# TensorE's sum over states moved to the front of a step with a lag of two units, and VectorE's gate one unit later

## The reference

```python
h = layernorm(x) @ W_fc1.T + b_fc1
u, z = split(h @ W_in.T)                    # 1024 channels each
u = silu(causal_conv4(u) + conv_b)
dt, B, C = split(u @ W_xproj.T)             # 32, 16, 16
delta = softplus(dt @ W_dt.T + b_dt)
h_t = exp(delta_t * A) * h_(t-1) + (delta_t * u_t) * B_t      # 16 states a channel
y_t = sum_over_states(h_t * C_t) + u_t * D
x = x + ((y * silu(z)) @ W_out.T) @ W_fc2.T + b_fc2
```

## Time and profile before

| | us |
|---|---|
| median of 3 runs | 4184.7 (4183.61 to 4185.17) |
| the profiled execution | 4190.9 |
| its span, from first to last instruction | 4189.1 |
| VectorE busy in it | 3739.9 (89%) |
| TensorE busy, as the profile models it | 3583.6 (86%) |
| GpSimd busy | 3318.2 (79%) |
| ScalarE busy | 2983.0 (71%) |

### The profile page before, as it was taken

One profiled execution on the slowest core, in us unless ns is written; L12 is line 12 of the kernel. 1 busy time (PEld: TensorE's weight loads), 2 busy tenths in 40 slices (PEclk: granted clock), 3 DMA queues, 4 the chain that ended last, 5 costly groups with the idle time before them and its releaser, 6 DMA issues. The chain is left out here.

```text
span 4189.1 us, 45303 instructions
## 1 busy us (share of the span) xinstructions
PE 3583.6 (86%) x11482; PEld 2027.0 (48%) x11482; DVE 3739.9 (89%) x3219; ACT 2983.0 (71%) x6359; POOL 3318.2 (79%) x1764
## 2 busy tenths in 40 slices
PE   7788888888888888888888888888888889888887
PEld 5545454445454455454445454445454445544443
DVE  0299999999999999999999999999999999998998
ACT  1477777777777777777777777777777777777774
POOL 0188888888788888888887888888888887878888
PEclk8899999999999999999999999999999999999999
DMA  2111011111011111011111011111001111101110
GB/s 90 53 50 52 12 48 46 52 52 52 12 47 46 52 52 52 11 52 44 50 52 52 16 48 43 49 52 52 31 33 43 50 52 52 45 19 43 46 46 8
DMA packets 48651, 183.79 MB, mean 44 GB/s; under 512 B 5274, under 2 KB 31138, under 8 KB 40002
## 3 DMA queue, kind: packets, MB, share of 16 engines
q1 hardware_dynamic: 46814, 174.16, 10.7%
q10 hardware_dynamic: 1636, 7.83, 0.5%
HBM read 164.14 MB, written 17.83 MB: 43 GB/s over the span
## 5 line engine op out<-in xcount | busy, mean ns | idle before, releaser
L387 POOL TENSOR_TENSOR st<-st,bc 128x1024 f32<-128x1024 f32 x1024 | 2401.9, 2358 | 645.8 <-DVE u L864 513.9
L653 PE MATMUL y_ps<-st,ident 128*128 128x512 f32 x4096 | 2041.7, 627 | 435.4 <-POOL st L387 433.0
L843 DVE TENSOR_TENSOR_SCAN st<-dec,st 128x1024 f32<-128x1024 f32 x1024 | 2325.8, 2279 | 84.2 <-ACT dec L444 80.2
L444 ACT ACTIVATE dec<-delta,decay 128x254 f32<-128x254 f32 x4096 | 1701.8, 466 | 724.4 <-DVE st L843 717.3
L653 PEld LDWEIGHTS y_ps<-st,ident 128*128 128x128 f32 x4096 | 758.5, 196 | 1279.2 <-POOL st L387 679.4
L831 DVE TENSOR_TENSOR st<-du,bc 128x1024 f32<-128x1024 f32 x800 | 964.6, 1206 | 15.2 <-ACT du L430 15.2
L371 POOL TENSOR_TENSOR st<-du_sb,bc 128x1024 f32<-128x1024 f32 x224 | 528.9, 2361 | 0.1
L864 DVE SCALAR_TENSOR_TENSOR u<-upad,chan,u 128x256 f32<-128x256 f32 x768 | 366.7, 519 | 6.8 <-ACT u L487 6.8
L694 PE MATMUL d_ps<-xnT,wxz 128*128 128x256 f32 x1024 | 250.5, 389 | 0.2
L706 PE MATMUL d_ps<-xnT,wxz 128*128 128x256 f32 x1024 | 244.0, 381 | 5.7 <-ACT zs L496 3.8
L694 PEld LDWEIGHTS d_ps<-xnT,wxz 128*128 128x128 f32 x1024 | 203.3, 199 | 91.4 <-issue 68.2
(11 more groups left out here) (102 smaller groups left out, 2936.4 us busy)
## 6 DMA issues: line engine op xcount, KB each, us to landing
bc<-bc_dram SPq DMA_DIRECT2D x64, 2048.0 KB, 9.1
xg<-x_dram SPq DMA_DIRECT2D x32, 256.0 KB, 2.8
x_dram<-xg SPq DMA_DIRECT2D x32, 256.0 KB, 2.0
last_x<-x_dram SPq DMA_DIRECT2D x32, 256.0 KB, 2.6
out_dram<-last_x SPq DMA_DIRECT2D x32, 256.0 KB, 2.2
bc<-w_inT_dram ACTq DMA_DIRECT2D x1, 4096.0 KB
adjt<-adjT_dram SPq DMA_DIRECT2D x32, 128.0 KB, 2.5
bc<-w_out_dram ACTq DMA_DIRECT2D x1, 2048.0 KB
```

The costliest lines, as they stand in the source:

```text
L387: nc.gpsimd.tensor_tensor(st[:, sl, :, :, :], st[:, sl, :, :, :], bc[:, p, 1, SU * q:SU * q + SU, None, :].to_broadcast([P, SU, 2, T]), AL ...
L444: a = nc.scalar.activation(dec[:, v % 2, s, j, :].rearrange("p (b t) -> p b t", b=PAIR)[:, :, 1:], delta[:, p, 2 * i + j, :].rearrange("p ...
L653: mm = nc.tensor.matmul(y_all, ident[:, :], st[:, sl, s, :, :].rearrange("p j t -> p (j t)"), start=False, stop=(q == Q - 1 and s == SU - ...
L843: nc.vector.tensor_tensor_scan(h, dec[:, v % 2, :, :, :].rearrange("p s j t -> p (s j t)"), h, 0.0, ALU.mult, ALU.add).then_inc(S["scanned ...
```

## The change

Three edits. `PE_LAG` goes from 1 to 2, so that step `v` of TensorE holds the sum of unit `v - 2`. The call of `state_sum` moves from the end of the step to its front. VectorE's gate moves from steps 2, 10, 18 and 26 to steps 3, 11, 19 and 27, at the same place within the step.

```diff
-PE_LAG = 1
+PE_LAG = 2
...
             def body(pe, k, p, scan, dense, ends, begins):
                 r = 1 - p
                 for v in range(U):
+                    if scan and v >= PE_LAG:
+                        state_sum(pe, k, p, v - PE_LAG)
+                    elif scan and has_previous(k):
+                        state_sum(pe, k - 1, r, v + U - PE_LAG)
                     if dense:
                         dense_pe(pe, k + 1, r, v, ends)
...
                     if scan:
                         if has_previous(k):
                             project_out(pe, k - 1, r, v, ends)
-                        if v >= PE_LAG:
-                            state_sum(pe, k, p, v - PE_LAG)
-                        elif has_previous(k):
-                            state_sum(pe, k - 1, r, v + U - PE_LAG)
...
                     if scan:
-                        if v % Q == 2 and v >= Q:
+                        if v % Q == 3 and v >= Q:
                             gate(dve, k, p, v // Q - 1)
-                        elif v % Q == 2 and has_previous(k):
+                        elif v % Q == 3 and has_previous(k):
                             gate(dve, k - 1, r, JP - 1)
                         scan_unit(dve, k, p, v)
```

## The result

The changed kernel took 4232.1 us (median of 4 runs, 4224.6 to 4233.4) against 4184.6 us, a ratio of 1.011 (95% interval 1.0098 to 1.0122): 47.5 us slower. I had forecast 4140 us, and the time lies outside my range. The span of its profiled execution is 4231.2 us, 42.1 more than before.

A forecast was written before the change was run, and what follows sets the result against it. VectorE bounds the kernel (89% busy), TensorE close behind (86%). Of 27 bodies 17 gain 1.6 us, 10 gain 0.5, 7 another 1.2: 1.5 us a body, 45 us over 30 bodies, 4184.7 to 4140; eight-in-ten range 4075 to 4200.

The forecast's parts named there:

- the side that I gave 0.18: Chance that the change is slower: 0.15 for late z projections plus 0.03 for clock falls.
- TensorE's edits: Lag and sum order on TensorE: same list of work, costed at 0, at most 12 us in all.
- The lead at step 3: Gate moved from step 2 to 3: VectorE runs 3.6 us earlier in some bodies, 2.5 in others.
- The gate of step 11: TensorE's sum 8 held for the gate; scan 16 still 1.6 or 0.5 us earlier.
- The gate of step 19: Sum 16 starts 9.5 us after scan 16, dt later; scan 16 to 29 takes 43.8 us in all bodies.
- The gate of step 27: Holds TensorE some 2 us more, covered by its 2.64 us idle for GpSimd shortly behind.
- The stretch from scan 29 to scan 16: Part of a body across the border: to take 79.4 to 80.0 us.
- the clock as a rival: Clock falls at the new stands, 1.7 us each at three gates a body: 4293 us, chance 0.03.
- the slower rival: TensorE stuck at step 11's gate delivers z projections late to ScalarE: up to 4241 us, chance 0.15.
- the slow form of scan 29 to scan 16: Stretch of 81.6 us against 79.9 in the fast form, put beside a clock fall at the body's border.
- the give of 1.9 us: ScalarE's slack ahead of scan 16's decays: about 0.6 us hold before L496 plus 1.33 us wait for VectorE.
- the 1.56 us gap: TensorE's only idle time between step 3 and past step 12, before 2357.78; could close as GpSimd is earlier.

The follow-up runs named there:

- pe_only: Kernel before with only TensorE's two edits (PE_LAG 2, sum at the front of the step), gates as before: 4188.6 us, +0.1.
- late3: Kernel before with only the gate of step 2 moved to step 3: 4074.1 us, -114.4.
- late11_fill: late11 with six products, their result overwritten, put into TensorE's stand ahead of the late gate: 4230.6 us, +44.9 to the kernel before.
- late11: Kernel before with only the gate of step 10 moved to step 11: 4321.4 us, +135.7.
- fill18: Kernel after with eight products, their result overwritten, on TensorE in step 18 ahead of sum 16: 4157.1 us, -31.5 to the kernel before.
- late3_27: Kernel before with the gates in steps 3, 10, 18 and 27: 4071.1 us, -114.6.
- late27: Kernel before with only the gate of step 26 moved to step 27: 4163.7 us, -22.0.
- fill2_18: fill18 with seven more such products on TensorE in step 2, ahead of sum 0: 4172.5 us, -13.1 to the kernel before.
- late19: Kernel before with only the gate of step 18 moved to step 19: 4191.0 us, +5.4.

## Why the prediction was wrong

The time came out slower, the side that I gave 0.18, and by a step that I had priced wrong. Step by step:

- **TensorE's edits cost nothing.** Right: `pe_only`, +0.1 us.
- **The lead at step 3.** Right. I had 3.6 or 2.5 us; the stretch 29 to 3 fell by 3.3 us in the kernel after (3.2 is the mean of my two), 3.8 in `late3`.
- **The gate of step 11.** The stand's price was right and the place too. From lead 3.6 to a gain of 1.6 at scan 16 is 2.0 us, and the stretch 11 to 16 grew by 2.0. Taken alone, my 1.9 us a body is `late11_fill`'s 2.0. In the kernel after the clock holds behind this stand, of 1.65 us in all 27 bodies; in `late11`, with 3.87 us, it does not.
- **The gate of step 19: the step that failed.** I put down that scan 16 to scan 29 would take 43.8 us. It took 9.4 + 16.8 + 19.5 = 45.7, 1.9 us a body more. The moment at which TensorE goes on behind the gate was right (9.5 us after scan 16, measured 9.55). Wrong was the duration of what follows it: I took L649 and the sum at full clock, though the earlier trace rows has a sum of 3.51 us behind an idle time of 2.64. So the term was the stretch 19 to 23: I had 14.3 us for it (43.8 less 9.5 and 20.0), and it took 16.8. With the clock kept up in `fill18` it is 14.55, and 16 to 29 is 43.45, within 0.4 of what I had.
- **The gate of step 27.** I had TensorE held 2 us more, covered by its idle time. It is held 3.4 us more (5.30 for 1.86), since an injection of 1.1 us goes ahead besides the scan of 2.2, and the cover held: the stretch 23 to 29 fell by 0.5.
- **The stretch from scan 29 to scan 16** I had at 79.8 us in the mean (17 of 80.0, 10 of 79.4). It took 22.2 + 36.6 + 21.8 = 80.6, 0.8 more. This is the clock as well: the nine bodies with half clock behind the stand of step 3 have 37.3 to 38.8 us from scan 3 to scan 11, the 18 others 35.9, and in `late3_27`, where 13 stands of 2.7 to 3.3 us are all passed at full clock, every body has 35.7.
- **The sum.** 1.9 + 0.8 = 2.7 us a body over 30 bodies is 81 of the 92 us between forecast and result; the rest is in the last bodies.
- **The rivals.** I had named the clock as a rival and given it 0.03, since the new stands would be "1 to 2 us". They are longer: 450.6 us in 127 stands, 3.5 in the mean, up to 8.3. I had priced each fall at 1.7 us in three places; it costs 2.2 us in step 19 (16.8 less 14.55), 1.4 to 2.9 in a third of the bodies in step 3, and nothing in step 27. I had counted from where TensorE stood before, and not asked how much earlier it would come when the waits ahead of it went. The Trainium skill, "TensorE: Matmul & The Clock Gate", section "What's actually happening", says that the clock goes by how busy the engine has recently been, and the traces agree: 0.50 to 0.69 behind stands of 3.1 to 4.9 us, and 1.00 where `fill18` has products in the stand. The mechanism of the slower rival, z projections late behind L649, exists as well; `late11` shows it with the clock's part on top. What decides is not only the lead, as I had it, but whether the clock falls behind the stand and what waits behind the slow matmuls.
- **What I misread in the rows.** The clock of 0.57 in the earlier trace rows is six sevenths of the window at 1.2 GHz, not half of it. And I took the fall at the border as the mark of the slow form of scan 29 to scan 16. The fast form has one too, 0.62 in the window from 2067 to 2071, at scan 29 (2067.24 in the earlier trace rows); what differs is the place of the fall.
- **What the changed profile should show.** VectorE's wait at gates was to fall to about 30 us (5.4), L649's to rise to 200 or more (450.6), scan 29 to 16 to take 79.4 to 80.0 (80.6), scan 16 to 29 to take 43.8 (45.7).
- **What the sign hung on.** A gain of 3.3 us at the gate of step 3 and losses behind those of steps 11 and 19. `late3` shows that the change holds one good edit, whose worth I under-read: with no late gate in step 11, the give of 1.9 us and the 1.56 us gap of my own working add up to 3.5, nearly the whole lead. In `late3` that gap and ScalarE's wait of 1.33 us are gone in all 27 bodies, scan 29 to scan 16 fell by 3.5 us, and a body by 3.8.

## What to carry to other kernels

When an instruction that another engine waits for is moved later, list what is queued behind that wait on the waiting engine, and move that work ahead of the wait first: with the pieces ahead of the first sum, the same four late gates went from +47.5 to -96.8 us. Move such things one at a time: here one of four gates was worth -114 us, one +136, and their sum hid both. And price a matmul behind a new stand at half clock, from a row of the same trace, before pricing it at full clock; then ask who waits for it, since a fall behind which nobody waits, as in step 27, costs nothing. Read the clock by stretches: the mean of the whole run fell in `late27`, which gained, and it says nothing of the place that matters.

## What the runs showed of the hardware that was not expected

Useless work made the kernel faster: six or eight products in a stand of TensorE took 91 us off `late11` and 79 us off the kernel after, by keeping the granted clock at 1.00 behind the stand and, in `late11_fill`, by moving the fall at the border. Where the clock fell, L649 with one sum took 4.4 to 5.3 us in the bodies shown, instead of 2.8. `fill2_18` shows the limit: where the stand is missing or short, such work is delay, and the time rose by 18 us.

The length of a stand alone did not decide whether the clock fell. Stands of 1.65 us in the kernel after were all passed at full clock, those of 4.8 and 5.3 us never. Between them both occur: in `late19` three stands of 2.0 us were followed by half clock and 24 of 0.8 to 2.9 us were not, in the kernel after nine of 3.0 to 4.0 us were and one of 3.02 was not, and in `late3_27` none of 13 from 2.7 to 3.3 us was.

And the place of a fall counts as much as its size. In the kernel before and `late11_fill` alike, half clock at scan 29 alone goes with 24.5 us from scan 29 to scan 3, and half clock with the pieces of step 0 with 26.0 to 26.2.
